# Attention walk: the scatter one-hots compared straight into their 32-bit ring on VectorE

## The chip, the cores and the metric

The kernel runs on one core of one Trainium2 chip. The metric is device time in microseconds of one execution; the time quoted is the median of several executions. The engines are TensorE (PE, with its weight loads as PEld), VectorE (DVE), ScalarE (ACT), GpSimd (POOL) and SyncE (SP, here only a DMA queue).

## What is computed

The program is a chain of four layers over 6250 nodes of 256 features: a graph attention layer, a mixture of experts with one expert per token, a two-step graph convolution with batch norm, and a second mixture with two experts per token. Only the first is touched:

```python
feat = (h @ W).reshape(N, H, D)                     # N = 6250, H = 4 heads, D = 64
el = einsum('nhd,hd->nh', feat, attn_l)
er = einsum('nhd,hd->nh', feat, attn_r)
e = leaky_relu(el[src] + er[dst], 0.2)              # 200000 edges, sorted by dst
ex = exp(e - segment_max(e, dst, N)[dst])
alpha = ex / segment_sum(ex, dst, N)[dst]
rst = segment_sum(feat[src] * alpha[..., None], dst, N)
out = elu(rst + bias)
```

## The kernel before

A first stage (the fill, to about 1300 us) counts the edges and, beside that, gathers a part of the source rows and keeps them in HBM. Then comes the **attention walk** (about 1300 to 2536 us), which the change is in. The edges, sorted by target, are cut into blocks of 256; a block and the tile of 128 target nodes that it meets form a pair. There are 832 pairs, walked in 52 turns of 16 (`UN`): a first turn, a loop over 50 and a last one, in which every engine runs its own instruction stream and is held to the others by semaphores alone.

For each pair `u`:

- SyncE (`walk_sp`) loads, broadcast over the partitions, the targets of two blocks (`load_row`), and for 7 pairs of 16 the kept source rows (`load`); GpSimd (`fetch_edges`, L710) gathers the rows of the other 9.
- VectorE (`make_turned`, L817) compares the targets of 256 edges with the partition's number: a one-hot with nodes on the partitions, 16-bit.
- TensorE (`spread`, L895) multiplies it with the nodes' attention terms; VectorE sums (`score_sum`, L827), adds the source's term (`score_left`, L837) and takes a maximum (`score_max`, L841).
- ScalarE (`weights`, L776, L779, L781) makes the exponentials, once into PSUM for VectorE and once into the message.
- VectorE (`messages`, L847) multiplies the gathered rows with the weights, 128x512 in 32 bits.
- VectorE (`make_onehot`, L809) compares, for two halves of 128 edges, each edge's target with the 128 node numbers: a one-hot with edges on the partitions, into `hot16`, a ring of four 16-bit buffers with the two halves interleaved. ScalarE (`widen`, L770) copies it, reordered, into `onehot`, a ring of eight (`GS`) 32-bit buffers.
- TensorE (`add_up`, L907 and L910) adds the product of the 32-bit one-hot and the messages to an accumulator in PSUM, and ScalarE (`collect`, L788) copies that to the target's tile.

The order on each engine is that of its loop body. VectorE's step `u` is: score sum of pair `u + 3`, message of `u + 1`, rest of the score of `u + 3`, one-hot of `u + 5`, score maximum of `u + 3`, turned one-hot of `u + 6`. ScalarE's is: weights of `u + 2`, widening of `u + 4`, collection of `u`. TensorE's is: add-up of `u`, spread of `u + 4`. At the beginning of a turn TensorE and ScalarE read the tile numbers of the turn from SBUF into registers (`tiles_of`). The one-hot of a pair waits (`s_up`) for the widening four pairs before it, the widening for the add-up (`s_a`) eight pairs before, the add-up for messages (`s_m`), exponentials (`s_den`) and the widened one-hot (`s_up`).

At the walk's start the last steps of the fill run out: VectorE clears a part of the arena (L638) and ScalarE the accumulators (L690); both raise `clear`, for which only ScalarE waits.

Of the kernel before, what the change touches and what calls it, by code (L numbers as in the profile page):

```python
# [18 lines left out]
BF16 = mybir.dt.bfloat16  # L19
F16 = mybir.dt.float16  # L20
# [6 lines left out]
P = 128  # L27
D = 256
# [4 lines left out]
TB = 7  # L33
# [10 lines left out]
UN = 16  # L44
GS = 8
RB = 4
# [10 lines left out]
PCOL = PCH * P  # L57
# [53 lines left out]
def wait(eng, sem, value):  # L111

    if isinstance(value, int) and value <= 0:
        return
    eng.wait_ge(sem, value)
# [21 lines left out]
def build(nc, x, src, dst, g0_w, g0_al, g0_ar, g0_bias, f0_gw, f0_gb, f0_w1, f0_b1, f0_w2, f0_b2,  # L137
# [18 lines left out]
    with ExitStack() as ctx:  # L156
        ctx.enter_context(nc.allow_non_contiguous_dma(reason="a few short index and bias loads"))

        def sb(name, shape, dt=F32):
            return ctx.enter_context(nc.sbuf_tensor(name, shape, dt))  # L160
# [3 lines left out]
        def sem(name):  # L164
            taken.append(nc.alloc_semaphore(name=name))
            return taken[-1]
# [16 lines left out]
        def room(width):  # L183
            used[0] += width
            return arena[:, used[0] - width:used[0]]

        acc_flat = room(NT * AW)
        acc = acc_flat.rearrange("p (t d) -> p t d", t=NT)
# [3 lines left out]
        onehot = room(GS * EB).rearrange("p (u j n) -> p u j n", u=GS, j=2)  # L192
# [35 lines left out]
        iota_n = sb("iota_n", [P, P])  # L228
        rings = sb("rings", [P, TB * (D + AW)])
# [53 lines left out]
        def pair_of(i, u):  # L283

            return UN // 2 * i + u // 2 + HALF * (u % 2)
# [67 lines left out]
        def count_plan():  # L353
# [193 lines left out]
            def attend():  # L547
                v_, pe_, t_ = (sem("cook_" + n) for n in ("v", "pe", "t"))
                mark = {}
                tag, gw, mw = "gat_walk", AW, MW  # L550
                s_oh, s_t, s_b, s_z, s_w, s_den, s_m, s_a, s_acc, s_c, s_one, s_low, s_up, s_near, s_lanes = (
                    sem(tag + "_" + n) for n in ("oh", "t", "b", "z", "w", "den", "m", "a", "acc", "c", "one", "low", "up",
                                                 "near", "lanes"))
                s_row = [sem(f"{tag}_row{r}") for r in range(NS)]
                s_g = {u: sem(f"{tag}_g{u}") for u in LIVE}
# [2 lines left out]
                s_st = [sem(f"{tag}_st{r}") for r in range(GS)]  # L558
                stores = [len(range(r, NKEPT, GS)) for r in range(GS)]
                near16 = rings[:, 0:PCOL].bitcast(F16)  # L560
                pair_lanes = rings[:, PCOL:PCOL + P].bitcast(F16).rearrange("p (n j) -> p n j", j=2)
                hot16 = rings[:, PCOL + P:PCOL + P + RB * P].bitcast(BF16).rearrange("p (r n j) -> p r n j", r=RB, j=2)
                assert PCOL + P + RB * P <= TB * D
                zt = small[:, :].rearrange("p (u j h) -> p u j h", u=RB, j=2)
                banks_e = [psum[2 + u % 2][:, 0:48].rearrange("p (j k h) -> p j k h", j=2, k=3) for u in range(UN)]
                banks_a = [psum[4 + 2 * (u % 2)] for u in range(UN)]
# [42 lines left out]
                clear = sem("clear")  # L609
# [82 lines left out]
                def final(i):  # L692
                    return isinstance(i, int) and i == STEPS - 1
# [69 lines left out]
                        steps(sp, body)  # L763

                def walk_act(act):
                        def widen(i, u):
                            n = UN * i + u
                            act.wait_ge(s_oh, n + 1)
                            wait(act, s_a, n - GS + 1)
                            act.copy(onehot[:, u % GS, :, :], hot16[:, u % RB, :, :].rearrange("p n j -> p j n")).then_inc(s_up, 1)  # L770

                        def weights(i, u):
                            n = UN * i + u
                            z = zt[:, u % RB, :, 0:4]
                            act.wait_ge(s_z, n + 1)
                            act.activation(z, z, ACT.Relu, scale=-1.0).then_inc(s_low, 1)  # L776
                            act.wait_ge(s_low, n + 1)
                            wait(act, s_m, n - 1)
                            act.activation(banks_w[u], z, ACT.Exp, scale=-1.0).then_inc(s_w, 1)  # L779
                            wait(act, s_a, n - RB + 1)  # L780
                            act.activation(msg[:, u % RB, :, D:GW], z, ACT.Exp, scale=-1.0).then_inc(s_den, 1)  # L781

                        def collect(i, u, t):
                            n = UN * i + u
                            act.wait_ge(s_a, n + 1)

                            wait(act, s_acc, n)
                            act.copy(arena[:, bass.ds(t * AW, mw)], banks_a[u][:, 0:mw]).then_inc(s_acc, 1)  # L788

                        for u in range(RB):  # L790
                            widen(0, u)
                        for u in range(2):
                            weights(0, u)
                        act.wait_ge(clear, 2)

                        def body(i):
                            tile = tiles_of(act, i * (UN // 4), UN // 4, mybir.EngineType.Activation, tpack_acc)
                            for u in range(UN):
                                if u + 2 < UN or not final(i):
                                    weights(i + (u + 2) // UN, (u + 2) % UN)  # L800
                                if u + RB < UN or not final(i):
                                    widen(i + (u + RB) // UN, (u + RB) % UN)
                                collect(i, u, tile(u))
                        steps(act, body)

                def walk_dve(dve):
                        def make_onehot(i, u):
                            wait(dve, s_up, UN * i + u - RB + 1)
                            dve.tensor_tensor(hot16[:, u % RB, :, :], pair_lanes,  # L809
                                              near16[:, bass.ds(2 * pair_of(i, u), 2)].unsqueeze(1).broadcast_to([P, P, 2]),  # L810
                                              ALU.is_equal).then_inc(s_oh, 1)

                        def make_turned(i, u):
# [30 lines left out]
                        def messages(i, u):  # L844
# [5 lines left out]
                                banks_w[u].unsqueeze(3).broadcast_to([P, 2, HEADS, HD]),  # L850
                                ALU.mult).then_inc(s_m, 1)

                        dve.memset(msg[:, :, :, GW:AW], 1.0).then_inc(s_one, 1)
                        dve.tensor_copy(pair_lanes, iota_n[:, :].unsqueeze(2).broadcast_to([P, P, 2])).then_inc(s_lanes, 1)
                        dve.wait_ge(s_lanes, 1)
                        for u in range(TR - 2):
                            make_turned(0, u)
# [30 lines left out]
                def walk_pe(pe):  # L888
                        def spread(i, u, t):

                            pe.wait_ge(s_t, UN * i + u + 1)

                            wait(pe, s_z, UN * i + u - 1)
                            for j in range(2):
                                last = pe.matmul(banks_e[u][:, j, :, :].rearrange("p k h -> p (k h)"),  # L895
                                                 onehot_t[:, u % TR, j * P:(j + 1) * P],
                                                 arena16[:, bass.ds(t * 24 + parts_at, 24)], start=True, stop=True)
                            last.then_inc(s_b, 1)

                        def add_up(i, u, other):  # L900
                            n = UN * i + u
                            pe.wait_ge(s_m, n + 1)
                            pe.wait_ge(s_den, n + 1)
                            pe.wait_ge(s_up, n + 1)

                            wait(pe, s_acc, n - 1)
                            pe.matmul(psum_all[:, bass.ds(other * 512 + mark_at[u], 1)], ident16[:, :], ident16[:, 0:1],  # L907
                                      start=True, stop=True, skip_group_check=True)
                            for j in range(2):
                                last = pe.matmul(banks_a[u][:, 0:mw], onehot[:, u % GS, j, :], msg[:, u % RB, j, 0:mw],  # L910
                                                 start=False, stop=False, skip_group_check=True)
                            last.then_inc(s_a, 1)

                        pe.wait_ge(copied, UNITS)
                        pe.wait_ge(s_one, 1)
                        early = pe.value_load(tpack[0:1, 0:1], min_val=0, max_val=(1 << 24) - 1)
                        for u in range(4):
                            spread(0, u, pe.snap((early // (1 << (6 * u))) % 64))

                        def body(i):  # L920
                            some = UN // 4 - (1 if final(i) else 0)
                            tile = tiles_of(pe, i * (UN // 4) + 1, some, mybir.EngineType.PE, tpack)
                            flags = pe.value_load(fresh[0:1, bass.ds(i, 1)], min_val=0, max_val=(1 << UN) - 1)
                            for u in range(UN):

                                add_up(i, u, pe.snap((flags // (1 << u)) % 2))
                                if u + 4 < UN or not final(i):
                                    spread(i + (u + 4) // UN, (u + 4) % UN, tile(u))
                        steps(pe, body)
# [1558 lines left out]
```

## Time and profile before

| what | value |
|---|---|
| median of 3 runs | 5615.69 us (5615.4 to 5622.19) |
| the profiled execution | 5624.17 us, span of the profile 5622.4 us |
| TensorE busy | 4452.0 us, 79% |
| VectorE busy | 3182.2 us, 57% |
| ScalarE busy | 2930.0 us, 52% |
| GpSimd busy | 2188.2 us, 39% |
| granted TensorE clock, mean | 0.894 |

The profile is of one execution. A busy share is a mean over stages that differ much, so a change inside one stage is read from that stage's own rows. Durations of neighbouring instructions on one engine overlap a little, as the start times show. A line such as L809 is a line of the kernel's source; the tile names are those of the large buffers that the rings are cut from (`arena` holds `onehot` and the messages, `rings` the 16-bit rings, `banks` is PSUM).

### The profile page before, as it was taken

What the parts mean: (1) busy time and instruction counts of PE and PEld (TensorE: products, weight loads), DVE (VectorE), ACT (ScalarE), POOL (GpSimd) and SP (SyncE); (2) the same over time, 40 slices, a digit from 0 to 9 for tenths busy, and PEclk for the clock granted to TensorE, in tenths of its full rate; (3) what the DMA queues carried; (4) which work ended last, traced back from release to release, by engine and by line L of the source; (5) the groups of instructions that cost most, each with busy time, mean ns of one, the idle gap of its engine ahead of it and who ended that gap; (6) DMA issues with size and microseconds to landing.
All of it is one profiled execution on the core that took longest, in us unless ns stands there. A gap on an engine that the chain in (4) does not pass through costs nothing. (4 is left out here: it accounts for less than half of the span.)

```text
span 5622.4 us, 113116 instructions
## 1 busy us (share of the span) xinstructions
PE 4452.0 (79%) x23524; PEld 3531.4 (63%) x23525; DVE 3182.2 (57%) x10258; ACT 2930.0 (52%) x7476; POOL 2188.2 (39%) x2057
## 2 busy tenths in 40 slices
PE   2566655557888888884799699998999963799997
PEld 1443332224666666664799478886788853799996
DVE  7698776667899899897445522225222245222222
ACT  0325566667777777776233355555555555233332
POOL 2477777776777777772222000000000006222221
PEclk9799877768999999995899899999999975899998
DMA  4367888887787777784566266663444444566665
GB/s 134 109 206 259 276 279 287 291 287 229 228 230 229 226 230 229 227 225 131 159 180 184 70 205 217 207 218 99 126 130 130 131 145 145 165 180 184 179 183 163
DMA packets 623736, 1084.57 MB, mean 193 GB/s; under 512 B 74390, under 2 KB 502093, under 8 KB 616748
## 3 DMA queue, kind: packets, MB, share of 16 engines
q1 hardware_dynamic: 504252, 733.75, 42.2%
q0 software_dynamic: 112144, 268.88, 17.9%
q10 hardware_dynamic: 7200, 80.28, 3.6%
q8 instruction: 61, 1.00, 0.1%
q14 instruction: 79, 0.65, 0.0%
HBM read 782.21 MB, written 309.57 MB: 194 GB/s over the span
## 5 line engine op out<-in xcount | busy, mean ns | idle before, releaser
L710 POOL DMA_INDIRECT arena<-table,arena x1664 | 1707.4, 1026 | 582.0 <-issue 456.6
L1378 PE MATMUL banks<-parts,a_wide 128*128 128x512 f32 x4900 | 1186.1, 401 | 17.7 <-ACT a_wide L1401 17.7
L1378 PEld LDWEIGHTS banks<-parts,a_wide 128*128 128x128 f32 x4900 | 926.1, 189 | 239.9 <-ACT a_wide L1401 18.5
L910 PE MATMUL banks<-arena 128*128 128x261 f32 x3328 | 998.9, 429 | 0.0
L656 PE MATMUL banks<-arena 128*128 128x392 bf16 x2368 | 612.3, 413 | 411.6 <-ACT banks L684 225.1
L1401 ACT CAST a_wide<-arena 128x896 fp32r<-128x896 f16 x700 | 659.1, 942 | 530.0 <-PE banks L1378 515.3
L2125 POOL DMA_INDIRECT expert_in<-arena,slot x147 | 160.3, 1090 | 1675.5 <-DVEq L2070 1633.7
L2308 ACT ACTIVATE rings<-banks,b_sb 128x128 f32<-128x128 f32 x1296 | 369.5, 368 | 828.6 <-PE banks L2341 828.6
L656 PEld LDWEIGHTS banks<-arena 128*128 128x128 bf16 x2368 | 340.2, 150 | 683.2 <-issue 642.4
L910 PEld LDWEIGHTS banks<-arena 128*128 128x128 f32 x3328 | 609.3, 204 | 60.5
L2204 POOL DMA_INDIRECT x_kept<-rings,idx_ring x162 | 251.4, 1552 | 978.7 <-DMA x_kept<-rings,idx_ring 772.6
L2341 PEld LDWEIGHTS banks<-yt_ring,arena 128*128 128x128 f32 x5184 | 609.0, 193 | 15.4 <-DVE yt_ring L2230 4.2
L2341 PE MATMUL banks<-yt_ring,arena 128*128 128x128 f32 x5184 | 610.3, 276 | 6.0 <-DMA arena<-in_L_ffn_W 2.0
L631 DVE TENSOR_TENSOR arena<-rings,arena 128x784 bf16<-128x784 f16 x1184 | 589.7, 559 | 0.0
L2352 PE MATMUL banks<-arena,rings 128*128 x2592 | 585.9, 379 | 0.0
L847 DVE TENSOR_TENSOR arena<-arena,banks 128x512 f32<-128x512 f32 x832 | 563.3, 677 | 0.5 <-ACT banks L779 0.5
L679 ACT CAST arena<-banks 128x1568 f16<-128x1568 f32 x200 | 292.9, 1465 | 432.0 <-PE banks L656 431.6
L2352 PEld LDWEIGHTS banks<-arena,rings 128*128 128x128 f32 x2592 | 480.0, 190 | 58.6
L788 ACT COPY arena<-banks 128x261 f32 x832 | 314.0, 377 | 242.3 <-PE banks L910 208.7
L1440 DVE TENSOR_TENSOR yt_ring<-yt_ring,banks 128x256 f32<-128x256 f32 x100 | 42.1, 421 | 649.6 <-ACT yt_ring L1406 649.6
L628 DVE TENSOR_TENSOR arena<-arena 128x1024 bf16<-128x1024 f16 x296 | 204.0, 689 | 255.3 <-PE banks L656 254.2
L770 ACT CAST arena<-rings 128x256 f32<-128x256 bf16 x832 | 325.3, 391 | 0.0
(355 smaller groups left out, 5186.5 us busy)
## 6 DMA issues: line engine op xcount, KB each, us to landing
arena<-counts SPq DMA_DIRECT2D x700, 224.0 KB, 2.5
arena<-in_L_ffn_W SPq DMA_DIRECT2D x114, 1024.0 KB, 5.1
edge_rows<-arena SPq DMA_DIRECT2D x364, 264.0 KB, 3.3
arena<-edge_rows SPq DMA_DIRECT2D x364, 264.0 KB
counts<-arena ACTq DMA_DIRECT2D x50, 1568.0 KB, 6.6
arena<-in_L_ffn_w SPq DMA_DIRECT2D x64, 1024.0 KB, 5.1
arena<-near_rows SPq DMA_DIRECT2D x416, 128.0 KB
expert_in<-rings SPq DMA_DIRECT2D x25, 2028.0 KB
```

Source lines behind the costliest of these rows:

```text
L631: last = dve.tensor_tensor(oh_k[:, p // KB % (OR // KB), :, :], keys16, kcols16[:, p:p + KB].unsqueeze(1).broadcast_to([P, KEYS, KB]), ALU ...
L656: last = pe.matmul(psum_all[:, bass.ds(bank, KEYS)], oh_b[:, p // LB % (OR // LB), :, p % LB], oh_k[:, p // KB % (OR // KB), :, p % KB], s ...
L710: pool.indirect_dma_start(out=got[:, r, j, :], out_offset=None, in_=table0, in_offset=bass.IndirectOffsetOnAxis(ap=src_sb[:, 2 * pair + j: ...
L770: act.copy(onehot[:, u % GS, :, :], hot16[:, u % RB, :, :].rearrange("p n j -> p j n")).then_inc(s_up, 1)
L788: act.copy(arena[:, bass.ds(t * AW, mw)], banks_a[u][:, 0:mw]).then_inc(s_acc, 1)
L847: dve.tensor_tensor(msg[:, u % RB, :, 0:D].rearrange("p j (h d) -> p j h d", h=HEADS), got[:, u % GS, :, 0:D].rearrange("p j (h d) -> p j ...
L910: last = pe.matmul(banks_a[u][:, 0:mw], onehot[:, u % GS, j, :], msg[:, u % RB, j, 0:mw], start=False, stop=False, skip_group_check=True)
L1378: last = pe.matmul(psum[u][:, 0:2 * D], a_wide[:, at:at + P], parts[:, a * 2 * D:(a + 1) * 2 * D], start=(a == 0), stop=(a == NT - 1))
L1401: act.copy(a_wide[:, w * CW:(w + 1) * CW], a_ring[:, c, :]).then_inc(o_cv, 1)
L2308: last = act.activation(hmid[:, u, c, :], psum[2 * u + h][:, (c % 4) * P:(c % 4 + 1) * P], func, bias=b1_sb[:, :, :].rearrange("p e c -> p ...
L2341: last = pe.matmul(psum[2 * u + h][:, (f % 4) * P:(f % 4 + 1) * P], w1_ring[:, u, c, f * P:(f + 1) * P], cols(yt_ring[:, u, :], c), start= ...
L2352: last = pe.matmul(psum[6 + u][:, 0:D], hmid[:, u, f, :], arena[:, bass.ds(e * FC * D + f * D, D)], start=(f == 0), stop=(f == FC - 1))
```

## The change

VectorE writes the one-hot directly into the 32-bit ring `onehot`, with the halves one after the other, and ScalarE's widening copy goes, with its semaphore `s_up` and the ring `hot16`. The node numbers to compare with (`pair_lanes`, now `lanes_two`) are laid out as two runs of 128. The one-hot waits for the add-up eight pairs before, and the add-up for the one-hot (`s_oh`). At the walk's start VectorE waits for both clears before it does anything.

```diff
-                pair_lanes = rings[:, PCOL:PCOL + P].bitcast(F16).rearrange("p (n j) -> p n j", j=2)
-                hot16 = rings[:, PCOL + P:PCOL + P + RB * P].bitcast(BF16).rearrange("p (r n j) -> p r n j", r=RB, j=2)
+                lanes_two = rings[:, PCOL:PCOL + P].bitcast(F16).rearrange("p (j n) -> p j n", j=2)
...
-                        def widen(i, u):
-                            n = UN * i + u
-                            act.wait_ge(s_oh, n + 1)
-                            wait(act, s_a, n - GS + 1)
-                            act.copy(onehot[:, u % GS, :, :], hot16[:, u % RB, :, :].rearrange("p n j -> p j n")).then_inc(s_up, 1)
...
-                        for u in range(RB):
-                            widen(0, u)
...
-                                if u + RB < UN or not final(i):
-                                    widen(i + (u + RB) // UN, (u + RB) % UN)
...
                         def make_onehot(i, u):
-                            wait(dve, s_up, UN * i + u - RB + 1)
-                            dve.tensor_tensor(hot16[:, u % RB, :, :], pair_lanes,
-                                              near16[:, bass.ds(2 * pair_of(i, u), 2)].unsqueeze(1).broadcast_to([P, P, 2]),
+                            wait(dve, s_a, UN * i + u - GS + 1)
+                            dve.tensor_tensor(onehot[:, u % GS, :, :], lanes_two,
+                                              near16[:, bass.ds(2 * pair_of(i, u), 2)].unsqueeze(2).broadcast_to([P, 2, P]),
                                               ALU.is_equal).then_inc(s_oh, 1)
...
+                        dve.wait_ge(clear, 2)
                         dve.memset(msg[:, :, :, GW:AW], 1.0).then_inc(s_one, 1)
-                        dve.tensor_copy(pair_lanes, iota_n[:, :].unsqueeze(2).broadcast_to([P, P, 2])).then_inc(s_lanes, 1)
+                        dve.tensor_copy(lanes_two, iota_n[:, :].unsqueeze(1).broadcast_to([P, 2, P])).then_inc(s_lanes, 1)
...
-                            pe.wait_ge(s_up, n + 1)
+                            pe.wait_ge(s_oh, n + 1)
```

## Rows read from the trace of the kernel before

**Rows 1.** Table of stretches: busy us (instructions) by engine, clock, DMA share, GB/s.

```profile
core 0: us, PE busy (x) PEld busy (x) DVE busy (x) ACT busy (x) POOL busy (x), PEclk, DMA share, GB/s
1315.86:2512.82 1196.96, 1032.15 (x5712) 766.85 (x5713) 1076.61 (x4900) 897.82 (x4081) 877.22 (x918) 0.94 0.79 229
1809.57:1832.05 22.48, 19.03 (x113) 14.24 (x113) 21.08 (x97) 17.57 (x80) 16.59 (x18) 0.99 0.79 234
1832.05:1855.87 23.82, 20.40 (x112) 15.19 (x113) 21.25 (x97) 17.66 (x80) 17.52 (x19) 0.93 0.79 227
```

**Rows 2.** Groups by line, 1280 to 2530 us: count, busy us, mean ns, idle before.

```profile
L847 DVE TENSOR_TENSOR arena<-arena,banks 128x512 f32<-128x512 f32 x830 | 562.0, 677 | 0.5 <-ACT banks L779 0.5
L770 ACT CAST arena<-rings 128x256 f32<-128x256 bf16 x832 | 325.3, 391 | 0.0
...
L809 DVE TENSOR_TENSOR rings<-rings 128x256 bf16<-128x256 f16 x832 | 236.6, 284 | 1.5 <-ACT arena L770 1.5
...
L907 PE MATMUL banks<-ident 128*128 128x1 bf16 x830 | 142.8, 172 | 168.0 <-ACT arena L770 106.1 <-DVE arena L847 10.1 <-ACT arena L781 3.3
```

**Rows 3.** Timeline of VectorE, one pair: start us, duration us, engine, line.

```profile
2476.13 0.28 DVE L817 TENSOR_SCALAR rings<-arena,number 128x256 bf16<-128x256 f16 x1
2476.33 0.20 DVE L827 TENSOR_REDUCE small<-banks 128x16 f32<-128x48 f32 x1
2476.44 0.67 DVE L847 TENSOR_TENSOR arena<-arena,banks 128x512 f32<-128x512 f32 x1
2477.04 0.16 DVE L837 TENSOR_TENSOR small<-small,arena 128x16 f32<-128x16 f32 x1
2477.12 0.28 DVE L809 TENSOR_TENSOR rings<-rings 128x256 bf16<-128x256 f16 x1
2477.33 0.15 DVE L841 TENSOR_TENSOR small<-small 128x8 f32<-128x8 f32 x1
2477.41 0.28 DVE L817 TENSOR_SCALAR rings<-arena,number 128x256 bf16<-128x256 f16 x1
```

**Rows 4.** Timeline of all engines at the beginning of one turn.

```profile
1805.37 0.67 DVE L847 TENSOR_TENSOR arena<-arena,banks 128x512 f32<-128x512 f32 x1
...
1807.24 0.20 PE L895 MATMUL banks<-arena,rings 128*128 x2
...
1809.57 0.17 PE L907 MATMUL banks<-ident 128*128 128x1 bf16 x1 [2.12 <-ACT arena L770]
...
1810.62 0.16 PE L907 MATMUL banks<-ident 128*128 128x1 bf16 x1
...
1810.90 0.21 DVE L827 TENSOR_REDUCE small<-banks 128x16 f32<-128x48 f32 x1 [1.14 <-PE banks L895]
```

**Rows 5.** Timeline of all engines at the beginning of the next turn.

```profile
1832.05 0.18 PE L907 MATMUL banks<-ident 128*128 128x1 bf16 x1 [2.12 <-ACT arena L770]
...
1834.07 0.17 PE L907 MATMUL banks<-ident 128*128 128x1 bf16 x1
...
1834.35 0.21 DVE L827 TENSOR_REDUCE small<-banks 128x16 f32<-128x48 f32 x1 [2.13 <-PE banks L895]
```

**Rows 6.** Groups by line, whole span: 32-bit operations of two operands, 128x256.

```profile
L1445 DVE TENSOR_TENSOR rings<-rings 128x256 f32<-128x256 f32 x96 | 40.1, 418 | 0.0
...
L2400 DVE TENSOR_TENSOR rings<-rings,arena 128x256 f32<-128x256 f32 x49 | 20.8, 425 | 1.7
```

**Rows 7.** Timelines of ScalarE and VectorE at the start of the walk.

```profile
1306.18 5.42 ACT L690 CAST arena<-rings 128x6272 f32<-128x6272 bf16 x1 [5.25 <-DMA counts<-arena]
...
1311.94 0.29 DVE L809 TENSOR_TENSOR rings<-rings 128x256 bf16<-128x256 f16 x1 [1.47 <-ACT arena L770]
...
1312.34 0.20 DVE L827 TENSOR_REDUCE small<-banks 128x16 f32<-128x48 f32 x1
```

**Rows 8.** Timeline of all engines at the beginning of the last turn.

```profile
2512.49 0.39 ACT L770 CAST arena<-rings 128x256 f32<-128x256 bf16 x1
...
2512.82 0.17 PE L907 MATMUL banks<-ident 128*128 128x1 bf16 x1 [1.42 <-ACT arena L781]
```

More of the change, by code:

```diff
@@ L550, in attend @@
                 tag, gw, mw = "gat_walk", AW, MW
-                s_oh, s_t, s_b, s_z, s_w, s_den, s_m, s_a, s_acc, s_c, s_one, s_low, s_up, s_near, s_lanes = (
-                    sem(tag + "_" + n) for n in ("oh", "t", "b", "z", "w", "den", "m", "a", "acc", "c", "one", "low", "up",
+                s_oh, s_t, s_b, s_z, s_w, s_den, s_m, s_a, s_acc, s_c, s_one, s_low, s_near, s_lanes = (
+                    sem(tag + "_" + n) for n in ("oh", "t", "b", "z", "w", "den", "m", "a", "acc", "c", "one", "low",
                                                  "near", "lanes"))
@@ L560, in attend @@
                 near16 = rings[:, 0:PCOL].bitcast(F16)
-                pair_lanes = rings[:, PCOL:PCOL + P].bitcast(F16).rearrange("p (n j) -> p n j", j=2)
-                hot16 = rings[:, PCOL + P:PCOL + P + RB * P].bitcast(BF16).rearrange("p (r n j) -> p r n j", r=RB, j=2)
-                assert PCOL + P + RB * P <= TB * D
+                lanes_two = rings[:, PCOL:PCOL + P].bitcast(F16).rearrange("p (j n) -> p j n", j=2)
                 zt = small[:, :].rearrange("p (u j h) -> p u j h", u=RB, j=2)
```

## The prediction

> **What bounds the kernel now.** The change touches only the attention walk, so the walk is read first, by the table of stretches: from the first pair's add-up to the last turn's there are 1196.96 us for 51 turns of the loop, 23.47 us a turn, in which VectorE is busy 1076.61 us (90%), TensorE 1032.15, ScalarE 897.82 and GpSimd 877.22 [rows 1]. No engine is full, so the share doesn't name the bound; the order of time within one pair does.
>
> In the timeline of VectorE one pair's six instructions start at 2476.13 (turned one-hot), 2476.33, 2476.44, 2477.04, 2477.12 and 2477.33, and the next pair begins at 2477.41 [rows 3]. That is 1.28 us a pair, with no idle time noted, although the six durations add up to 1.74: neighbours overlap by some 0.08 us, and what counts is start to start. The one-hot (L809) lasts 0.28 and holds VectorE for 0.21 (2477.12 to 2477.33); the message (L847) lasts 0.67 and holds it for 0.60. So sixteen pairs want 20.5 us of VectorE and take it back to back. TensorE needs less when nothing holds it: two add-ups follow each other 1.05 us apart, at 1809.57 and 1810.62 [rows 4]. ScalarE's widening copy (L770, 391 ns) lies in 0.39 us a pair of an engine that is busy 17.57 of a turn's 22.48 [rows 1, 2]. In the middle of a turn the pace is VectorE's.
>
> The rest of a turn is its beginning. TensorE stands still from the spread at 1807.24 until 1809.57, then does an add-up and the spread for which VectorE's score sum (L827) has waited 1.14 us, until 1810.90 [rows 4]. This turn lasted 22.48 us at a granted clock of 0.99; the next one lasted 23.82 at 0.93, because its first pairs ran at 1.2 GHz (2.02 us from 1832.05 to 1834.07 instead of 1.05) and VectorE waited 2.13 us there [rows 1, 5]. The mean of 23.47 says that about three turns in four are of the second kind: (23.47 − 22.48) / (23.82 − 22.48) = 0.74.
>
> **The change part by part.**
>
> *The price of the new comparison.* Now 832 one-hots of 128x256, 16-bit in and out, take 284 ns each [rows 2]. Afterwards the output is 32-bit. No row shows a comparison with 16-bit inputs and a 32-bit output. The nearest rows are VectorE operations of two SBUF operands, 128x256, in 32 bits: 418 ns (L1445) and 425 ns (L2400) [rows 6]; at the other end stands L809's own 284 ns, if only the inputs' width counted. The 512 elements of a message need 0.60 us of start to start, 1.2 ns each with its fixed part; the one-hot's 256 need 0.21, 0.8 ns each [rows 3]. So the width is worth about a factor of two on this engine, and the wide operand decides in every row that has one. I take 418: 0.134 us more a pair, bounds 0 and 0.141. A price below nothing is excluded: the element count stays 256 and nothing becomes narrower. The new order of the operands (innermost index repeated for the one operand) is that of the message, whose weight is repeated over 64 columns. 832 × 0.134 = 111.5 us of VectorE, bounds 0 and 117.
>
> The Trainium skill, page "VectorE: DVE Perf Modes", section "What auto-detection actually checks", has two results per cycle only where every tensor of the instruction is 16-bit, so that a mixed form falls to one. Its 0.96 GHz gives an estimate of 128 cycles = 0.133 us more, and a sum of 111 instead of 111.5; no run here shows the mixed form, and this is the one place that speaks on it.
>
> *What of it lies on the path.* In the middle of a turn all of it: nothing waits ahead of L809, and score maximum, turned one-hot, score sum and message are queued behind it. At a turn's beginning some is covered. Between the message that lets TensorE into the last add-up of a turn (1805.37) and the score sum that waits (1810.90), VectorE makes three one-hots; their 3 × 0.134 = 0.40 us fit into the 1.14 us of idle time [rows 4]. Where the first pairs run at 1.2 GHz VectorE waits for TensorE pair by pair, 2.02 against 1.28; with 1.41 it would wait 0.13 less in each of the one or two pairs concerned, some 0.2 more [rows 3, 5]. So a turn takes back 0.40 to 0.62, 51 turns 20 to 32, of which I take 26.
>
> *The copy that goes.* 832 × 391 ns = 325 us leave ScalarE [rows 2]. I cost this at nothing. What hides it: the copies run four pairs ahead of the add-up that reads them, and VectorE's message (L847) has waited for ScalarE's weights only 0.5 us in the whole walk [rows 2]. If the cover weren't there, it would show as idle time of L847, and it doesn't.
>
> *The waits.* The one-hot waits for the add-up of three pairs before (8 buffers, made 5 pairs ahead). In VectorE's order the score sum ahead of it needs a spread that TensorE issues after a later add-up, so this wait is always over: nothing. TensorE's add-up waits for VectorE's one-hot in place of the copy; it was made five pairs earlier: nothing. No DMA moves, and no queue is passed.
>
> *The wait at the start.* VectorE now waits for both clears before its first instructions of the walk. In the trace it had four one-hots and five turned ones behind it, and stood 1.47 us until 1311.94 for the first copy, which followed ScalarE's clear (1306.18 + 5.42 = 1311.60); the first score sum came at 1312.34 [rows 7]. Afterwards six turned one-hots at 0.20, five one-hots at 0.21 + 0.13 and about 0.3 for the two preparations start at 1311.60: 3.2 us, first score sum at 1314.8. Queued behind are the first scores, and ScalarE's weights and TensorE's add-up wait for them. Cost 2.5 us, once; bounds 0 (if the engines behind find the time again) and 3.2.
>
> *Sum.* 111.5 − 26 + 2.5 = 88 us. Against the profiled execution's own 5624.17 (span 5622.4 and 1.8 around it) that is 5712; the median of the runs is 8.5 lower, 5615.69, and what is added doesn't depend on that difference: 5703.
>
> **The rivals.**
>
> *More half-clock turns.* TensorE's idle time in each pair grows from 1.28 − 1.05 = 0.23 to 0.36. Granted clock fell to 1.2 GHz where TensorE had stood still for 2.1 us at a turn, and not in the middle of turns with their short gaps [rows 1, 4, 5]. If the quarter of turns that are spared now are hit too, 13 × 1.34 = 17 us come on top; if half of all turns got a second stretch, 34 more. Then 5720 to 5754. For it: more idle time in all. Against it: single gaps stay below 0.4 us. The Trainium skill, page "TensorE: Matmul & The Clock Gate", section "Part 1: The HAM clock gate (the "warmup" mystery)", calls half rate the default that recent activity lifts; that speaks for this rival, and rows 1 agree as far as the standstill goes.
>
> *The half clock goes away.* A longer turn shifts the standstill against what the clock follows. With every turn spared, 38 × 1.34 = 51 us are given back: 5652. For it: one turn in four is spared already, after the same standstill, so the clock doesn't follow from its length alone. Against: the standstill stays 2.1 us long and the gaps beside it grow.
>
> *TensorE really waits for the copy.* The profile puts 106.1 us of TensorE's waits, 50 times, down to L770 [rows 2]; the change takes that releaser away. If it were the cause, all VectorE idle time at turns would go, and VectorE alone would set the turn: 21.08 busy + 2.14 = 23.22 instead of 23.47, 51 × 0.25 = 13 saved, with the start 5605: not slower. It decides if the add-up at a turn follows the end of a copy. The page puts the wait down to it because a copy ended shortly before, but TensorE and ScalarE both restart there with loads of their own, of fixed length; and at the last turn, where fewer words are loaded, the add-up starts at 2512.82 while the copy ahead of it, begun at 2512.49, ends only at 2512.88 [rows 8]; and by the code the copy that the add-up needs is four pairs older. So hardly.
>
> *It does not slow VectorE.* If the comparison keeps 284 ns, only the start is left: 5618.
>
> **How the numbers follow.** The forecast, VectorE pays and a quarter of it is covered, 0.76; more half clock 0.09; less half clock 0.07; TensorE freed 0.04; no price 0.04. Predicted 5703. The forecast alone spans 5686 (32 covered, and nine more turns spared: 111.5 − 32 + 2.5 − 12) to 5736 (nothing covered, price 0.141, start 3.2). The range reaches to the rivals of the clock on both sides: 5650 to 5740; it leaves out the free comparison and the freed TensorE, 0.08, and the worst of the clock. About 0.2% (11 us) is what a measurement of this kernel can tell from no change. Faster by more than that: half of the freed TensorE, 0.02. Within: its other half and the free comparison, 0.06. Slower: 0.92.
>
> **What would show it.** Right: the one-hot's row at 410 to 430 ns; one pair of VectorE 1.41 us from start to start; a turn of 24.2 at full clock (22.48 + 2.14 − 0.40) and 25.3 otherwise (23.82 + 2.14 − 0.62); the score sum's idle time at turns down by some 0.4 us each; ScalarE's busy time in a turn down by 6.3. Wrong: a one-hot row near 284; a pair that stays at 1.28; TensorE's standstill of 2.1 us at turns gone; granted clock of the walk other than about 0.94; another stage longer or shorter by more than a few us.

## The result, and the profile after

| | before | after |
|---|---|---|
| median, us | 5618.5 (5615.4 to 5622.19, 4 runs) | 5693.03 (5688.16 to 5698.97, 4 runs) |
| ratio | | 1.0127, 95% interval 1.0115 to 1.0139 |
| profiled execution: span, us | 5622.4 | 5697.2 |

The change makes the kernel slower, by 74.5 us (71 by the ratio). 5703 was predicted, in a range of 5650 to 5740, counted from the median of three runs, 5615.69; a fourth run moved it to 5618.5.

The walk after the change, first by the table of stretches (columns as in [rows 1]): all 51 turns from the first add-up to the last turn's, then one turn at full clock and one with the half clock.

```profile
1320.25:2585.63 1265.38, 1023.93 (x5713) 762.12 (x5713) 1175.61 (x4899) 697.09 (x3265) 943.93 (x919) 0.95 0.76 216
1517.74:1541.81 24.07, 19.03 (x113) 14.24 (x114) 22.97 (x97) 13.73 (x64) 18.59 (x19) 1.00 0.79 224
1813.72:1839.90 26.18, 21.67 (x112) 16.04 (x113) 23.15 (x97) 13.64 (x64) 18.66 (x19) 0.88 0.73 202
```

A turn takes 24.81 us (1265.38 / 51) where it took 23.47 [rows 1]. VectorE is busy for 93% of the walk instead of 90%, ScalarE for 55% instead of 75%: the copy is gone, and the turn is longer all the same.

The groups by line, 1280 to 2640 us, that answer to [rows 2]; the numbers of the lines have moved, L797 is the one-hot, L835 the message, L815 the score sum, L896 the first instruction of an add-up:

```profile
L708 POOL DMA_INDIRECT arena<-table,arena x942 | 968.4, 1028 | 351.2 <-issue 197.6 <-DVE arena L835 147.6 <-DMA edge_rows<-arena 6.0
L835 DVE TENSOR_TENSOR arena<-arena,banks 128x512 f32<-128x512 f32 x832 | 559.7, 673 | 0.5 <-ACT banks L771 0.5
L797 DVE TENSOR_TENSOR arena<-rings 128x256 f32<-128x256 f16 x832 | 342.7, 412 | 0.0
...
L815 DVE TENSOR_REDUCE small<-banks 128x16 f32<-128x48 f32 x832 | 164.0, 197 | 90.4 <-PE banks L884 85.5
...
L896 PE MATMUL banks<-ident 128*128 128x1 bf16 x832 | 143.3, 172 | 245.7 <-DVE arena L835 130.6 <-DVE arena L797 110.0 <-ACT arena L773 1.8
```

In the kernel before, the same view has for the gathers and for the score sum:

```profile
L710 POOL DMA_INDIRECT arena<-table,arena x938 | 897.2, 956 | 348.7 <-issue 235.7 <-DVE arena L847 110.2 <-DMA edge_rows<-arena 2.8
...
L827 DVE TENSOR_REDUCE small<-banks 128x16 f32<-128x48 f32 x832 | 168.3, 202 | 118.8 <-PE banks L895 107.1 <-issue 11.0
```

The one-hot takes 412 ns instead of 284, and VectorE stands idle before score sums for 90.4 us of the walk instead of 118.8. TensorE's 2.2 us waits at the beginnings of turns are still there, 110.0 us of them; they are now put down to VectorE's one-hot, as they were put down to ScalarE's copy before. VectorE's timeline of one pair, which answers to [rows 3]:

```profile
1525.92 0.28 DVE L805 TENSOR_SCALAR rings<-arena,number 128x256 bf16<-128x256 f16 x1
1526.11 0.20 DVE L815 TENSOR_REDUCE small<-banks 128x16 f32<-128x48 f32 x1
1526.23 0.67 DVE L835 TENSOR_TENSOR arena<-arena,banks 128x512 f32<-128x512 f32 x1
1526.82 0.17 DVE L825 TENSOR_TENSOR small<-small,arena 128x16 f32<-128x16 f32 x1
1526.91 0.41 DVE L797 TENSOR_TENSOR arena<-rings 128x256 f32<-128x256 f16 x1
1527.24 0.16 DVE L829 TENSOR_TENSOR small<-small 128x8 f32<-128x8 f32 x1
1527.32 0.28 DVE L805 TENSOR_SCALAR rings<-arena,number 128x256 bf16<-128x256 f16 x1
```

1.40 us from turned one-hot to turned one-hot, where it was 1.28. Only one interval differs: from the one-hot to the score maximum, 0.33 instead of 0.21.

The beginning of a turn at full clock, all engines, to be held against [rows 4]:

```profile
1541.81 0.17 PE L896 MATMUL banks<-ident 128*128 128x1 bf16 x1 [2.25 <-DVE arena L797]
...
1542.86 0.16 PE L896 MATMUL banks<-ident 128*128 128x1 bf16 x1
...
1543.14 0.21 DVE L815 TENSOR_REDUCE small<-banks 128x16 f32<-128x48 f32 x1 [1.02 <-PE banks L884]
```

TensorE stands about as long as it did (2.25 us, it was 2.12), and an add-up still takes 1.05 us. And the start of the walk, which answers to [rows 7]:

```profile
1308.11 5.42 ACT L688 CAST arena<-rings 128x6272 f32<-128x6272 bf16 x1 [8.86 <-DMA counts<-arena]
...
1313.60 0.09 DVE L842 MEMSET arena<- 128x32 f32 x1 [6.93 <-ACT arena L688]
...
1316.75 0.20 DVE L815 TENSOR_REDUCE small<-banks 128x16 f32<-128x48 f32 x1
...
1320.25 0.18 PE L896 MATMUL banks<-ident 128*128 128x1 bf16 x1 [1.83 <-ACT arena L773]
```

From the end of ScalarE's clear (1313.53) to the first score sum there are 3.22 us; there were 0.74.

So the 74.8 us between the two spans divide up: 1.9 before the walk (the fill's last stores landed later in this execution), 2.5 at its start (from the clear to the first add-up 6.7 instead of 4.3), 68.4 in the 51 turns (1265.38 − 1196.96), 2.0 behind them. Nothing outside the walk carries it.

To see where the 68.4 come from, the intervals from start to start of VectorE's instructions were summed over the 51 turns, from every row of its timeline:

| interval | before, us | after, us | difference |
|---|---|---|---|
| one-hot → score maximum | 166.1 | 274.2 | +108.1 |
| turned one-hot → score sum (with the waits at turns) | 295.3 | 269.8 | −25.5 |
| score maximum → turned one-hot | 77.1 | 64.6 | −12.5 |
| the three others | 658.3 | 656.8 | −1.5 |

The one-hot costs 108.1 us, and 39.5 of them are given back elsewhere.

The 25.5 us are of two kinds, which the granted clock of each turn tells apart (mean of the turns; the interval is that from turned one-hot to score sum, summed over a turn from 2.6 us before its first add-up, so that its own waits are in it):

| turns at a granted clock of | before: turns, us a turn, interval | after: turns, us a turn, interval |
|---|---|---|
| 0.99 to 1.00 | 8, 22.63, 4.82 | 17, 24.08, 4.58 |
| 0.87 to 0.94 | 43, 23.63, 5.97 | 34, 25.18, 5.63 |

A turn of the same kind gives back 0.24 or 0.33 us in this interval, some 16 us in all. The other 10 come from nine more turns in which the clock doesn't fall.

### The profile page after: what moved, and what is told of

It is laid out like the page before. It is cut to its first block and busy times, and to the rows that moved or that the text cites. A ratio compares the mean times of both kernels' runs of the same rounds, so it can differ in the third digit from the quotient of the medians.

```text
span 5697.2 us, 111210 instructions
## 1 busy us (share of the span) xinstructions
PE 4433.9 (78%) x23524; PEld 3523.9 (62%) x23525; DVE 3280.4 (58%) x10258; ACT 2726.8 (48%) x6644; POOL 2264.6 (40%) x2057
## 5 line engine op out<-in xcount | busy, mean ns | idle before, releaser
L708 POOL DMA_INDIRECT arena<-table,arena x1664 | 1779.8, 1070 | 583.0 <-issue 417.2
L835 DVE TENSOR_TENSOR arena<-arena,banks 128x512 f32<-128x512 f32 x832 | 559.7, 673 | 0.5 <-ACT banks L771 0.5
L797 DVE TENSOR_TENSOR arena<-rings 128x256 f32<-128x256 f16 x832 | 342.7, 412 | 0.0
```

Source lines behind the costliest of these rows:

```text
L708: pool.indirect_dma_start(out=got[:, r, j, :], out_offset=None, in_=table0, in_offset=bass.IndirectOffsetOnAxis(ap=src_sb[:, 2 * pair + j: ...
L797: dve.tensor_tensor(onehot[:, u % GS, :, :], lanes_two, near16[:, bass.ds(2 * pair_of(i, u), 2)].unsqueeze(2).broadcast_to([P, 2, P]), ALU ...
L835: dve.tensor_tensor(msg[:, u % RB, :, 0:D].rearrange("p j (h d) -> p j h d", h=HEADS), got[:, u % GS, :, 0:D].rearrange("p j (h d) -> p j ...
```

## The experiments

Turns are given as in the prediction: from the first add-up of the walk to that of the last turn, divided by 51. The two ways by which the copy could have mattered were tried first.

### The copy alone: put back where it was taken away, taken away where it was

The changed kernel with a ScalarE copy of the old form, in the old place, that nobody reads:

```diff
+                        def widen(i, u):
+                            act.wait_ge(s_oh, UN * i + u + 1)
+                            wait(act, s_up, UN * i + u - 1)
+                            act.copy(unread[:, u % 2, :, :],
+                                     near16[:, 0:EB].rearrange("p (n j) -> p j n", j=2)).then_inc(s_up, 1)
```

> The changed kernel, with a ScalarE copy of the removed form (128x256, 16-bit to 32-bit) put back in the place of the old one, into a buffer that nobody reads; the output is unchanged. Theory (VectorE sets the pace, the removed copy was hidden): the same time as the changed kernel, 5693 us within 10, and a turn of the walk of 24.8 us. Rival (the relief of ScalarE gave some of the price back, which is why 73 us were measured and not the full 832 x 0.128 = 106): up to 33 us slower than the changed kernel, 5726, a turn of 25.4.

Measured: 5690.41 us (ratio to before 1.0132, interval 1.0105 to 1.0159), a turn of 24.78. The same as without the copy (5693.03), to 0.1%. Its groups by line, 1330 to 2500 us, show that the copy was really there:

```profile
L810 DVE TENSOR_TENSOR arena<-rings 128x256 f32<-128x256 f16 x756 | 314.6, 416 | 0.0
L788 ACT CAST rings<-rings 128x256 f32<-128x256 f16 x755 | 295.2, 391 | 0.0
```

The relief of ScalarE, 391 ns a pair, is worth nothing that can be measured.

The other way about, the kernel before without its copy, but with its 16-bit comparison:

```diff
-                            wait(dve, s_up, UN * i + u - RB + 1)
+                            wait(dve, s_oh, UN * i + u - RB + 1)
                             dve.tensor_tensor(hot16[:, u % RB, :, :], pair_lanes,
...
-                            pe.wait_ge(s_up, n + 1)
+                            pe.wait_ge(s_oh, n + 1)
...
-                        for u in range(RB):
-                            widen(0, u)
+                        act.wait_ge(clear, 2)
+                        act.copy(onehot.rearrange("p u j n -> p (u j n)"),
+                                 eps[:, 0:1].broadcast_to([P, GS * EB])).then_inc(s_up, 1)
```

> The kernel before with its 16-bit comparison kept and the widening copy left out, with the waits of the changed kernel; TensorE adds up with a constant in the 32-bit ring, so the aggregation of the attention layer is left out. Theory (the width of the comparison is the whole price, the copy was hidden): as before plus the 2.5 us of the start, 5621 us within 10, a turn of 23.5 us. Rival (TensorE waited 2.1 us a turn for the copy): that wait goes, a turn of 21.1 to 22 us, 5515 to 5545.

Measured: 5625.98 us (ratio 1.0011, interval 1.0 to 1.0021), a turn of 23.50. The groups by line, 1330 to 2500 us:

```profile
L801 DVE TENSOR_TENSOR rings<-rings 128x256 bf16<-128x256 f16 x797 | 228.9, 287 | 0.1
...
L900 PE MATMUL banks<-ident 128*128 128x1 bf16 x796 | 137.2, 172 | 163.3 <-DVE rings L801 99.3 <-DVE arena L839 11.0 <-ACT arena L775 6.4
```

Without any copy TensorE waits about as long at turns as before; the profile just names another instruction that happened to end shortly ahead. The rival that TensorE waits for the copy falls, and the new comparison is the whole loss. What in it costs the time isn't taken apart: its output is 32-bit, and the order of its operands is new as well (the innermost index now repeats one operand 128 times), and no run has the one without the other.

### TensorE's standstill at turns, and what it covers

Both kernels with TensorE's loads of tile numbers spread over the turn:

```diff
-                            some = UN // 4 - (1 if final(i) else 0)
-                            tile = tiles_of(pe, i * (UN // 4) + 1, some, mybir.EngineType.PE, tpack)
...
                                 if u + 4 < UN or not final(i):
-                                    spread(i + (u + 4) // UN, (u + 4) % UN, tile(u))
+                                    if u % 4 == 0:
+                                        tile = tiles_of(pe, i * (UN // 4) + 1 + u // 4, 1, mybir.EngineType.PE, tpack)
+                                    spread(i + (u + 4) // UN, (u + 4) % UN, tile(u % 4))
```

> The kernel before with TensorE's four loads of packed tile numbers per turn no longer all at the turn's beginning but one by one, each ahead of the first spread that needs it. Theory (TensorE stands still for its own loads): the standstill falls from 2.1 us to about 0.7, VectorE's idle time at turns goes, and no stretch at 1.2 GHz follows: a turn of 21.1 us if VectorE alone sets it, about 22 if GpSimd's 18 gathers of 0.96 us and 0.25 us between them do; 5615 minus 75 to 120, so 5500 to 5545. Rival (TensorE waits for the copy): a turn stays at 23.5, 5618.

> The changed kernel with the same loads spread over the turn. Theory (part of the price was covered by VectorE's idle time at turns): without that idle time VectorE sets every turn, 24.07 - 1.01 = 23.1 us, 5693 - 51 x 1.75 = 5604; and against the kernel before with the same edit the change then costs 16 x 0.124 = 2.0 us a turn, 100 us in all, if that one is set by VectorE, or about 55 if GpSimd sets that one. Rival (the cover lies elsewhere): the same 73 us between the two as without the edit.

Measured: the kernel before with this edit 5589.18 us (ratio 0.9944, interval 0.9926 to 0.9961), a turn of 22.83; the changed kernel with it 5658.23 us (ratio 1.0064, 1.0043 to 1.0086), a turn of 24.12. TensorE's standstill at turns, 2.12 us before, is now:

```profile
1355.49 0.20 PE L895 MATMUL banks<-arena,rings 128*128 x2
1356.59 0.17 PE L907 MATMUL banks<-ident 128*128 128x1 bf16 x1 [0.90 <-ACT arena L788]
```

So 1.2 of the 2.1 us were TensorE's loads of tile numbers; the other 0.9 remain, with the load of the flags that stayed at the beginning, and aren't taken apart. The first edit is faster than both kernels, by 0.6% of the kernel before. But both gained less than expected, and the difference between the two stayed at 1.29 us a turn. The groups by line, 1330 to 2480 us, of the kernel before with the edit, then of the changed one, say why:

```profile
L710 POOL DMA_INDIRECT arena<-table,arena x907 | 874.3, 964 | 276.5 <-issue 221.2 <-DVE arena L847 55.3
L827 DVE TENSOR_REDUCE small<-banks 128x16 f32<-128x48 f32 x806 | 164.9, 205 | 15.1 <-issue 9.1 <-PE banks L895 3.7
L837 DVE TENSOR_TENSOR small<-small,arena 128x16 f32<-128x16 f32 x806 | 136.5, 169 | 56.0 <-DMA arena<-table,arena 55.1
```

```profile
L708 POOL DMA_INDIRECT arena<-table,arena x858 | 889.7, 1037 | 261.6 <-issue 170.9 <-DVE arena L835 90.7
L825 DVE TENSOR_TENSOR small<-small,arena 128x16 f32<-128x16 f32 x764 | 128.1, 168 | 40.6 <-DMA arena<-table,arena 39.5
```

The score sum's waits for TensorE are gone (3.7 us in all), and in their place VectorE waits for gathered rows, 55.1 us and 39.5. GpSimd's gathers, with the gaps between them, take (874.3 + 276.5) / 907 = 1.27 us each, 22.84 for the 18 of a turn; in the changed kernel it is (889.7 + 261.6) / 858 = 1.34, and 24.15. Busy and idle time together make up the turn on any engine, so these sums don't name the bound; VectorE's waits do, and the next runs, in which fewer gathers make the turn shorter. GpSimd now shares in the pace of both.

So the full price of the comparison could be seen only with GpSimd out of the way, which leaving out half of its gathers does:

```diff
-                                fetch(pool, u % GS, pair_of(i, u), s_g[u])
+                                fetch(pool, u % GS, pair_of(i, u), s_g[u], 1)
...
-                                dve.wait_ge(s_g[u], 32 * (i + 1))
+                                dve.wait_ge(s_g[u], 16 * (i + 1))
```

> The kernel before with one of the two gathers of each of the 9 pairs that GpSimd serves in a turn left out (the other half of the rows is stale). Theory (VectorE sets the pace, GpSimd's 18 gathers hide below it): a turn of 23.5 us as before. Rival (GpSimd's gathers share in the pace of the kernel before): a shorter turn, down to 22.5.

> The changed kernel with the same gathers left out. Theory: a turn of 24.8 us as with them. Rival (the gathers, which last 1.03 us instead of 0.96 since the change, carry a part of the loss): a turn of 24.1 or less.

> The kernel before with TensorE's loads spread over the turn and the same gathers left out, so that neither TensorE's standstill nor GpSimd can set the turn. Theory: VectorE's own work alone, 21.1 us a turn.

> The changed kernel with both of these edits. Theory: VectorE's own work alone, 23.1 us a turn; against the kernel before with both edits the change costs its full price, 16 x 0.124 to 0.128 = 2.0 us a turn and 101 to 104 us over 51 turns, where 1.34 us a turn were measured without the edits. Rival (the price is less than the durations say, and nothing was covered at turns): the same 1.3 us a turn as without the edits.

| turn, us | before | after | difference |
|---|---|---|---|
| as they are | 23.47 | 24.81 | 1.34 |
| half of the gathers | 23.40 | 24.76 | 1.36 |
| loads spread | 22.83 | 24.12 | 1.29 |
| loads spread, half of the gathers | 21.31 | 22.88 | 1.58 |

With the gathers halved alone, the two kernels keep their turns (5619.44 and 5693.81 us in all): GpSimd shares in the pace of neither. With both edits a turn is 21.31 and 22.88 us, 5508.09 and 5599.06 us in all. The first meets its expectation of 21.1 nearly, the second lies below its 23.1, and the price is 1.58 us a turn, between the 2.0 of the theory and the 1.3 of its rival. The same sums of intervals tell what is missing: the one-hot's interval grew from 164.6 to 273.4 us, +108.8 or 2.13 a turn, the full price; the interval up to the score sum fell from 189.1 to 173.5, 0.31 a turn, a rest of cover at turns (probably the gap at the loop's own branch: what is left of VectorE's idle time before score sums has no engine named for it); and the interval ahead of the turned one-hot fell again, from 77.6 to 65.2, 0.24 a turn.

### What waited ahead of the turned one-hot

This last gain stands in every pair of kernels, with the copy and without it. By the code the turned one-hot waits there for SyncE's transfer of the targets' rows. The kernel before with those rows loaded for eight pairs only, once:

```diff
-                        for v in range(2):
+                        for v in range(NS):
                             load_row(0, v)
...
-                                if u % 2 == 0 and (u + 4 < UN or not final(i)):
-                                    v = u // 2 + 2
-                                    load_row(i + v // (UN // 2), v % (UN // 2))
...
-                            dve.wait_ge(s_row[v % NS], 16 * (UN // 2 // NS * i + v // NS + 1))
+                            dve.wait_ge(s_row[v % NS], 16)
```

> The kernel before with the broadcast rows of targets loaded for the first eight pairs only, so that the turned one-hot waits for no transfer any more (the later pairs compare with the rows of the first ones, and the attention terms are wrong). It asks where the 0.016 us a pair went that VectorE lost before the turned one-hot and no longer loses since the change (from the score maximum's start to the turned one-hot's start 0.0945 us on the mean before, 0.079 after). If the turned one-hot waited for the rows: 0.079 here too, and a turn shorter by 0.25 us. If the time is lost in VectorE's own supply of instructions: 0.094 as before.

Measured: that interval fell from 77.1 to 64.0 us over the 51 turns, to what the changed kernel has (64.6), and the turn from 23.47 to 23.18; the other intervals stayed. The whole came to 5619.59 us (one execution), only 4.6 less than the profiled execution before: the 51 turns are 14.6 us shorter, but 4.0 more lie ahead of them and 6.1 behind. So VectorE did wait for these rows in the kernel before. The waits stand at fixed pairs of a turn: on the mean 0.11 us ahead of pair 8, 0.06 ahead of pair 0 and 0.04 ahead of pair 6, each the first of two that share a transfer (0.04 more ahead of pair 1, which needs no new rows by the code, stay open). Pair 8 of one turn of the kernel before, 0.19 us from start to start instead of 0.08:

```profile
1813.18 0.16 DVE L841 TENSOR_TENSOR small<-small 128x8 f32<-128x8 f32 x1
1813.37 0.29 DVE L817 TENSOR_SCALAR rings<-arena,number 128x256 bf16<-128x256 f16 x1
```

Most of it shows as no idle time (the walk's turned one-hots have 2.0 us of it), because it lies inside the duration of the instruction ahead. With the longer pair these waits are gone.

### The wait at the start

The changed kernel with VectorE's wait for the clears moved behind all but the last of the preparing comparisons:

```diff
-                        dve.wait_ge(clear, 2)
...
                         for u in range(TR - 2):
+                            if u == TR - 3:
+                                dve.wait_ge(clear, 2)
                             make_turned(0, u)
```

> The changed kernel with VectorE's wait for the two clears moved behind the first five turned one-hots and the five one-hots, to the one instruction that needs it. Theory (the wait at the start costs 2.5 us because ten comparisons stand behind it): from the end of ScalarE's clear to the first score sum 0.3 to 0.5 us instead of 3.2, and the first add-up 4.0 to 4.3 us after the clear, as before the change, instead of 6.7. Rival (another engine sets the start): the first add-up stays 6.7 us behind the clear. The turns as in the changed kernel.

Measured, by the timeline of all engines:

```profile
1301.25 5.42 ACT L688 CAST arena<-rings 128x6272 f32<-128x6272 bf16 x1 [6.87 <-DMA counts<-arena]
...
1306.90 0.20 DVE L815 TENSOR_REDUCE small<-banks 128x16 f32<-128x48 f32 x1
...
1310.47 0.18 PE L897 MATMUL banks<-ident 128*128 128x1 bf16 x1 [1.80 <-ACT arena L773]
```

From the end of the clear at 1306.67 it is 0.23 us to the first score sum and 3.8 to the first add-up, instead of 3.2 and 6.7. The comparisons behind the wait are what the start costs. In the whole time (5694.72 us, one execution) 3 us can't be seen. Its turns weren't quite those of the changed kernel: 24.98 us on the mean, with 12 at full clock instead of 17.

## Why the prediction was right

*VectorE paces the middle of a turn.* Right: a pair grew from 1.28 to 1.40 us (1.41 forecast), by the one-hot alone, and putting the copy back or taking it away moved nothing.

*The price.* 0.134 us a pair was taken, between 0 and 0.141. The interval behind the one-hot grew by 108.1 us over 816 pairs, 0.132. The nearest rows, of the same shape with 32 bits on all sides [rows 6], gave it, although the inputs stayed 16-bit: the new comparison runs as slowly as these. That the wide output alone decides is not shown, since the new order of the operands came with it; the prediction let the order pass because the message has it too, but the message is 32-bit throughout and can't tell. The rows that it read for the width don't give "about a factor of two" either: 1.2 against 0.8 ns an element is 1.5, and none of its wide rows has a narrow input. The 418 that it took doesn't rest on this. This is the mixed form that no run had shown. The Trainium skill, page "VectorE: DVE Perf Modes", section "What auto-detection actually checks", gives two results per cycle only if every tensor is 16-bit and is read or written with a step of one, so the new form falls to one result per cycle by the output, and by the repeated operand as well; at 412 ns against 418 and 425 the trace agrees.

*The cover at turns.* 26 us were taken, from 0.40 to 0.62 a turn; the interval that holds these waits gave back 25.5. That the two agree is luck. In turns of the same kind the cover was 0.24 and 0.33 us, some 16 us; 10 came from the clock, which the sum had at nothing. In the turns shown at full clock the idle time before the score sum fell from 1.14 to 1.02, and the one at the loop's branch, 0.23 us before, is no longer noted:

```profile
1808.12 0.21 DVE L827 TENSOR_REDUCE small<-banks 128x16 f32<-128x48 f32 x1 [0.23 <-issue]
```

A full-clock turn came to 24.07 (24.2 forecast).

*What was not foreseen* is the 12.5 us ahead of the turned one-hot. "No DMA moves" was true and not enough: VectorE waited for a transfer that the change doesn't touch, and a slower pace hides it. The prediction took the mean pair at its undisturbed 1.28 us, though the turns' 21.1 us of work are 1.32 a pair; the difference was there to be asked about. Without these 12.5 the forecast of 88 would have been 75.5 against 74.5 measured, but that nearness, too, hangs on the cover and the clock making up 26 between them.

*The start.* 2.5 forecast, 2.5 measured, and its cause shown.

*The rivals.* TensorE waiting for the copy: excluded by the kernel without a copy. The clock: both rivals happened in part. Of the 51 turns, 17 now keep a granted clock of 1.00 where 8 had 0.99 or 1.00, and 7 fall to 0.90 or below (26.18 us at 0.88 in the one shown) where 1 did; the mean granted clock of the walk is 0.95, it was 0.94, and the nine turns gave back some 10 us. So the forecast was wrong on turns of the second kind: 43 of 51 were hit before, not three in four, and 34 after. The count goes with the comparison in most runs: with the 16-bit one it is 8 without the copy and 7 with half of the gathers, with the new one 17 with the copy put back and 16 with half of the gathers. But it isn't fixed: it is 12 of 51 with the rows loaded once and 12 with the later wait at the start, each read from one trace. The Trainium skill's page "TensorE: Matmul & The Clock Gate", section "Part 1: The HAM clock gate (the "warmup" mystery)", calls half rate the default and has activity lift it, which would speak for more half clock with an idler TensorE; on the mean no run here shows that, although TensorE's idle time in an undisturbed pair grew from 0.23 us (1.28 − 1.05) to 0.35 (1.40 − 1.05). No price at all: excluded by the one-hot's row.

The score sum's waits fell less at full clock than the 0.4 us that was named as a sign, and ScalarE's busy time in a full-clock turn fell by 3.8 us (17.57 to 13.73), not 6.3: its busy time counts overlapping instructions once, and the durations themselves add up to 6.3 less (21.66 to 15.36).

## What to carry to other kernels

Work moved from an engine with slack to the one that paces the loop is paid for there, and what the other engine is spared buys nothing back (here 108 us against a copy worth nothing); which engine paces is read from the starts of its instructions in the middle of the loop, not from busy shares. A releaser that the profile names for a wait may only have ended near by: ask what the instruction needs by the code, or take the releaser away. And a slower pace can give something back wherever the pacing engine itself was waiting for others, in short waits too that lie inside the instruction ahead.

## What the runs showed of the hardware

**A gather on GpSimd takes longer when it starts under the new comparison of VectorE.** The gathers of the walk lasted 956 ns on the mean before and 1028 after, 1028 with the copy put back and 955 in the kernel with the 16-bit comparison and no copy, so it goes with the comparison and not with the copy. In the changed kernel's timeline of all engines:

```profile
1342.28 0.41 DVE L797 TENSOR_TENSOR arena<-rings 128x256 f32<-128x256 f16 x1
1342.43 1.10 POOL L708 DMA_INDIRECT arena<-table,arena  x1 [0.31 <-DVE arena L835]
...
1343.69 0.41 DVE L797 TENSOR_TENSOR arena<-rings 128x256 f32<-128x256 f16 x1
1343.83 1.10 POOL L708 DMA_INDIRECT arena<-table,arena  x1 [0.30 <-issue]
...
1346.63 0.95 POOL L708 DMA_INDIRECT arena<-table,arena  x1 [0.30 <-issue]
```

A gather that starts 0.14 us after a one-hot's start takes 1.10 us, one that starts elsewhere 0.95. Of the 917 gathers in the 51 turns, the 407 that began about 0.1 us after a one-hot's start average 1.11 and those that began 0.6 us after it or later 0.95. In the kernel before, 141 began about 0.1 us after the 16-bit one-hot's start, and they average 0.98. The Trainium skill, page "SBUF — State Buffer", section "SBUF: two separate sides", has VectorE and GpSimd exclude each other at a shared port, among others while VectorE reads two inputs from SBUF, as the one-hot does, and GpSimd reads from SBUF too, as the gather does with its row numbers; the rows agree in kind, though the wait it would cause shows only as a longer gather, by 0.15 us. It costs this kernel nothing as long as GpSimd has time to spare; with the loads spread it has none, and then 18 gathers of 1037 ns instead of 964, 1.31 us a turn, are as much as the 1.29 by which the two kernels differ.

**Register loads at the beginning of a turn stop TensorE.** With four words of tile numbers and one of flags loaded there it stands still for 2.12 us; with the four words loaded one by one, behind work already issued, it stands for 0.90. VectorE then hardly waits for TensorE any more (3.7 us in the view above), and the granted clock of the walk rises from 0.94 to 0.99. Where the clock falls after the standstill, that comes on top: of the two turns of the changed kernel shown, one takes 26.18 us at a mean clock of 0.88 and the other 24.07 at 1.00.
